# A depthwise convolution and a rotation, each behind a group norm: order of late loads, order of GpSimd's work, place of small matrix products, and a tile without padding

## The chip, the cores and the metric

One core of one Trainium2 chip. The metric is the device time of one execution in microseconds (us), the median of several runs. The kernel is written by hand for five engines: PE (TensorE), DVE (VectorE), ACT (ScalarE), POOL (GpSimd) and SP (SyncE, which here only issues DMAs). They meet in semaphores alone.

## The reference, cut to what matters

```python
x = x + conv5x5_depthwise(group_norm(x), kernel(weight))   # x: (16, 128, 64, 64) f32, pad 2, 32 groups of 4 channels
x = x + einsum('hvc,bchw->bvhw', R, group_norm(x))         # R: (64, 128, 128), one matrix per image row h
```

The group norm takes mean and variance over 4 channels and one whole image, so the second norm of a group can be had only when the first line is done for that group, and the rotation mixes all 128 channels, so it begins when all 32 groups are done.

## The kernel before

**First stage: 32 groups of four channels.** A group holds 4 channels of 16 images. On the 128 partitions lie the 64 rows of images 0 to 7 (low half) and of images 8 to 15 (high half); the free dimension is image, channel, column. The vertical part of the convolution is a banded 64x64 matrix (`taps`), one per channel and per column offset d of 0 to 4; the horizontal part is the shift of the moving operand by d. So `convolve(k, pair, d)` (L560) issues four matrix products of 64x64 by 512 columns for a pair of channels, one in each quadrant of the array, and five offsets add up in PSUM: 2 pairs x 5 offsets x 4 products in a group. The profile shows each f32 product as two records, so 80 records in a group. The moving operand is `padded` (L91), images of 68 columns with two columns of zeros on each side, which four memsets at the start (L308 to L310) write once.

The steps run s = -3 to 34 on all engines, each with its part of several groups:

- SP loads x for group s+5 (`load_half`, L196: 8 DMAs of 128 KB, in pieces of 256 bytes) into a ring of 7 once `x1_ready` frees the slot; after steps 11, 18 and 25 of its loop it stores norms (`store_norms`, L228), and at steps ROT_STEP = 24 to 27 it issues one fourth of the rotation matrices each (L253 to L256, 1 MB each).
- DVE measures group s+3 (`measure`, L484, four `bn_stats` at L489), from step FILL = 4 on ahead of the rest of the step and before that behind it; makes scale and shift of group s+1 (L509, L511); adds the second pair of group s-1 to x (`add`, L473: L478 reads PSUM, L481 reads two SBUF tiles) and measures the sum (L496); makes the variance term of round s+2 (`dev`, `dev2`, `spread`, L522 to L527); adds the first pair of group s.
- PE convolves group s, and between its products puts the small products that average over partitions: `average_spread(s+1)` (L578, the variance) at the first two offsets of the first pair, `average_mean(s+2)` (L584) in the second pair, at the first two offsets, or the last two while 0 <= s < FILL. PE takes instructions in order, so a small product that waits holds all behind it.
- ACT takes the root (L418), normalises five of the eight image pairs (L423), evicts two channels of each group (L407) and stores the sum of a group as two DMAs of 512 KB on its own queue (L207).
- POOL builds the banded matrices of group s+2 (`spread_taps`, L327, four instructions at L339, one per channel) and normalises the other three image pairs (`normalise`, L349, three instructions at L354). From step FILL on it does the four matrices first.

**Between the stages.** Once the sums of groups 0 to 27 are stored (the waits at L265), SP loads the first seven units of the second stage for these 112 channels (`early`, L266 to L269: 7 DMAs of 896 KB). It stores the last group (L272), waits until all sums are stored (L276), and loads the remaining 16 channels of these units (`late`, L282). All of SP's DMAs go through one queue, in order; ACT's stores go through another.

**Second stage.** 32 units of 4 image rows: load (L301), normalise (ACT L448, POOL L383, DVE L539 for the first unit), one 128x128 by 512 product per row (PE L632), add to x (DVE L549), store as 15 DMAs of 2 MB and two of 1 MB (L287). PE's own turning of the rotation matrices (L617) starts when they have landed (L608).

Of the kernel before, what the change touches and what calls it, by code (L numbers as in the profile page):

```python
# [10 lines left out]
B, C, H, W = 16, 128, 64, 64  # L11
GC = 4
# [7 lines left out]
PAD = 2  # L20
WP = W + 2 * PAD
# [39 lines left out]
ROT_STEP = GROUPS - 8  # L61

def conv_rotate_kernel(nc, x, weight, rota, out):
# [5 lines left out]
    with ExitStack() as ctx:  # L70
# [20 lines left out]
        padded = [piece((GC, J, WP)) for _ in range(GRING)]  # L91
# [214 lines left out]
        def _(pool):  # L306
            nc.gpsimd.memset(eps[:], EPS).then_inc(consts_ready, 1)
            for t in padded:  # L308
                nc.gpsimd.memset(t[:, :, :, 0:PAD], 0.0).then_inc(consts_ready, 1)
                nc.gpsimd.memset(t[:, :, :, W + PAD:WP], 0.0).then_inc(consts_ready, 1)  # L310
# [16 lines left out]
            def spread_taps(k):  # L327
# [5 lines left out]
                if k >= TRING:  # L333
                    pool.wait_ge(convolved, 2 * (k - TRING + 1))
                of_rows = mask[:].rearrange("p (b r) -> p b r", r=TAPS)
                for c in range(GC):
                    at = (k * GC + c) * KW
                    of_taps = row_taps[:, :, at:at + KW].rearrange("p r d -> p d r")
                    last = nc.gpsimd.tensor_tensor(  # L339
                        taps[k % TRING][:, c * KW:(c + 1) * KW].rearrange("p d (b r) -> p d b r", r=TAPS),  # L340
                        bass.AP(tensor=of_rows.tensor, offset=of_rows.offset,
                                ap=[of_rows.ap[0], [0, KW], *of_rows.ap[1:]]),
                        bass.AP(tensor=of_taps.tensor, offset=of_taps.offset,
                                ap=[*of_taps.ap[:2], [0, BLOCKS], of_taps.ap[2]]),
                        ALU.mult)
                    if c % 2 == 1:
                        last.then_inc(taps_ready, 1)

            def normalise(k):  # L349
# [3 lines left out]
                for j in range(POOL_J):  # L353
                    last = nc.gpsimd.tensor_scalar(padded[k % GRING][:, :, j, PAD:PAD + W], xin[k % XRING][:, j],  # L354
# [10 lines left out]

            for s in STEPS:
                if group(s + 1) and 0 <= s < FILL:
                    normalise(s + 1)
                if group(s + 2):
                    spread_taps(s + 2)  # L370
                if group(s + 1) and s >= FILL:
                    normalise(s + 1)
                if s - 3 in range(LAST, GROUPS):
                    send_norms(s - 3)
# [14 lines left out]
        def _(act):  # L389
# [21 lines left out]
            for s in STEPS:  # L411
# [7 lines left out]
                if group(s + 1):  # L419
                    k = s + 1  # L420
                    act.wait_ge(affine_ready, k + 1)
                    for j in range(POOL_J if k else 0, J):
                        last = nc.scalar.activation(padded[k % GRING][:, :, j, PAD:PAD + W], xin[k % XRING][:, j],  # L423
# [130 lines left out]
        def _(pe):  # L554
            pe.wait_ge(consts_ready, 1 + 2 * GRING)
# [4 lines left out]
            def convolve(k, pair, d):  # L560
                bank = 2 * ((2 * k + pair) % PAIRS)
                if d == 0:
# [5 lines left out]
                    if 2 * k + pair >= PAIRS:  # L568
                        pe.wait_ge(y_ready, (2 * k + pair - PAIRS + 1) * 2)
                        pe.wait_ge(own_ready, 2 * k + pair - PAIRS + 1)  # L570
                for rows, half, c in ((low, low, 0), (low, high, 1), (high, low, 1), (high, high, 0)):
                    last = nc.tensor.matmul(ps[half, bank + c], taps[k % TRING][rows, (2 * pair + c) * KW + d, 0:H],  # L572
                                            padded[k % GRING][rows, 2 * pair + c, :, d:d + W],
                                            start=(d == 0), stop=(d == KW - 1))
                if d == KW - 1:
# [17 lines left out]

            for s in STEPS:
                first = KW - 2 if 0 <= s < FILL else 0
                for d in range(KW):
                    if group(s):
                        convolve(s, 0, d)
                    if is_round(s + 1) and d < 2:
                        average_spread(s + 1, high if d else low)  # L600
                for d in range(KW):
                    if group(s):
                        convolve(s, 1, d)
                    if is_round(s + 2) and d in (first, first + 1):
                        average_mean(s + 2, low if d == first else high)
# [55 lines left out]
```

## Time and profile before

| | us |
|---|---|
| median of 3 runs | 499.12 (496.28 to 499.28) |
| the profiled execution, its own time | 498.91 |
| its span, first to last instruction | 497.1 |
| PE busy | 425.3 |
| DVE busy | 369.6 |
| ACT, POOL busy | 259.2, 256.6 |

The span is told in microseconds from the first instruction. The mean granted clock of PE is 0.949 of full speed. The page's slices of PE show it at 1.0 in most of the first stage. Busy shares are averages over both stages; what bounds the kernel has to be read stage by stage.

### The profile page before, as it was taken

How to read it: one execution, taken by the hardware profiler on the slowest of the kernel's cores; microseconds unless marked ns; L12 is line 12 of the kernel's file. 1: busy time of each engine (PE TensorE's matmuls, PEld its weight loads, DVE VectorE, ACT ScalarE, POOL GpSimd, SP SyncE). 2: the span in 40 equal slices, each digit the busy share in tenths (PEclk: the TensorE clock that was granted, in tenths of full speed). 3: DMA queues.
4: the chain of work that ended last, by engine and by line, in shares of the span. 5: the costliest groups of instructions: out<-in, count | busy, mean ns of one | idle time of the engine just before them, and what ended most of it. 6: DMA issues, size and time to landing. Idle time of an engine off the chain costs nothing.

```text
span 497.1 us, 8820 instructions
## 1 busy us (share of the span) xinstructions
PE 425.3 (86%) x3168; PEld 229.9 (46%) x3168; DVE 369.6 (74%) x716; ACT 259.2 (52%) x502; POOL 256.6 (52%) x348
## 2 busy tenths in 40 slices
PE   0199979999999999999999959945999979788972
PEld 0145535556655666556665535523444434333430
DVE  3419999999999999999999856663777643355462
ACT  1344536565565655656556535424777746364640
POOL 3484586675766757667576634213344423132320
PEclk9999998999999999999999979975999989798987
DMA  9989999999999999899999998996999999999998
GB/s 135 182 181 229 211 211 233 249 236 245 250 216 250 230 243 258 210 248 220 244 241 275 273 246 223 341 339 97 390 411 419 407 415 417 415 415 414 415 404 282
DMA packets 180443, 140.70 MB, mean 283 GB/s; under 512 B 139760, under 2 KB 141872, under 8 KB 176304
## 3 DMA queue, kind: packets, MB, share of 16 engines
q1 hardware_dynamic: 159264, 106.86, 76.8%
q10 hardware_dynamic: 20656, 33.16, 23.6%
q8 instruction: 25, 0.41, 0.3%
q0 software_dynamic: 480, 0.11, 0.2%
q14 instruction: 18, 0.15, 0.1%
HBM read 72.96 MB, written 67.15 MB: 282 GB/s over the span
## 4 chain that ended last, share of the span: by engine, by line
DVE 44%; PE 23%; DMA 22%; issue 4%; SPq 2%; POOL 1%; ACTq 1%; ACT 0%; POOLq 0%; DVEq 0%
DMA out_dram<-area 18%; PE ps L572 14%; DVE stats L489 12%; DVE stats L496 12%; DVE area L481 9%; PE ps L632 8%; DVE area L478 4%; DVE area L549 2%; SPq L198 2%; DMA tap_rows<-line 2%; DVE dev L525 1%; DMA area<-in_x_dram 1%; DVE affine L511 1%; DVE affine L509 1%; DMA area<-tap_rows 1%
## 5 line engine op out<-in xcount | busy, mean ns | idle before, releaser
L572 PE MATMUL ps<-area 64*64 64x512 f32 x2560 | 292.7, 607 | 3.9 <-POOL area L339 3.9
L572 PEld LDWEIGHTS ps<-area 64*64 64x64 f32 x2560 | 160.5, 134 | 92.8 <-issue 54.9
L339 POOL TENSOR_TENSOR area<-mask,area 128x325 f32<-128x325 f32 x128 | 130.3, 1054 | 76.5 <-PE ps L572 71.4
L632 PE MATMUL ps<-area 128*128 128x512 f32 x256 | 123.6, 635 | 20.4 <-DVE area L549 16.0
L549 DVE TENSOR_TENSOR area<-ps,area 128x512 f32<-128x512 f32 x128 | 82.9, 687 | 61.3 <-DMA out_dram<-area 46.2
L407 ACT ACTIVATE area<-ps 64x512 f32<-64x512 f32 x128 | 75.8, 592 | 72.1 <-PE ps L572 69.8
L448 ACT ACTIVATE area<-area,norm 128x256 f32<-128x256 f32 x157 | 80.5, 588 | 55.8 <-PE ps L632 54.1
L423 ACT ACTIVATE area<-area,affine 128x256 f32<-128x256 f32 x163 | 83.7, 590 | 42.0 <-DVE affine L511 42.0
L383 POOL TENSOR_SCALAR area<-area,norm 128x256 f32<-128x256 f32 x95 | 52.0, 562 | 91.7 <-PE ps L632 88.5
L489 DVE BATCH_NORM_STATS2 stats<-area 128x6 f32<-128x512 f32 x128 | 80.4, 690 | 18.1 <-DMA area<-in_x_dram 18.1
L632 PEld LDWEIGHTS ps<-area 128*128 128x128 f32 x256 | 50.2, 204 | 82.8 <-issue 48.0
L496 DVE BATCH_NORM_STATS2 stats<-area 128x6 f32<-128x512 f32 x128 | 80.7, 693 | 1.1
L354 POOL TENSOR_SCALAR area<-area,affine 128x256 f32<-128x256 f32 x93 | 64.1, 702 | 27.2 <-DVE affine L511 27.2
L481 DVE TENSOR_TENSOR area<-area 128x512 f32<-128x512 f32 x64 | 59.8, 934 | 0.0
L478 DVE TENSOR_TENSOR area<-ps,area 128x512 f32<-128x512 f32 x64 | 43.6, 682 | 0.0
L589 PE MATMUL ps<-stats,half_mean 64*64 64x16 f32 (+1 forms) x144 | 17.2, 200 | 28.6 <-DVE affine L511 16.0
L589 PEld LDWEIGHTS ps<-stats,half_mean 64*64 64x64 f32 x144 | 18.9, 142 | 45.5 <-issue 30.6
L418 ACT ACTIVATE std<-ps,eps 128x16 f32<-128x16 f32 (+1 forms) x36 | 9.8, 273 | 50.7 <-PE ps L581 34.7
L581 PEld LDWEIGHTS ps<-spread,half_mean 64*64 64x64 f32 x144 | 18.2, 140 | 26.6 <-issue 15.0
L581 PE MATMUL ps<-spread,half_mean 64*64 64x16 f32 (+1 forms) x144 | 16.7, 198 | 8.0 <-DVE spread L527 8.0
L509 DVE RECIPROCAL affine<-std 128x16 f32<-128x16 f32 (+1 forms) x36 | 8.2, 227 | 15.1 <-ACT std L418 15.1
L362 POOL DMA_DIRECT2D norm<-affine x8 | 4.1, 521 | 20.1 <-DVE affine L511 19.8
(27 smaller groups left out, 68.7 us busy)
## 6 DMA issues: line engine op xcount, KB each, us to landing
area<-in_x_dram SPq DMA_DIRECT2D x252, 128.0 KB, 4.3
x_scratch<-area ACTq DMA_DIRECT2D x62, 512.0 KB, 6.2
out_dram<-area SPq DMA_DIRECT2D x15, 2048.0 KB, 17.9
area<-x_scratch SPq DMA_DIRECT2D x25, 1024.0 KB, 14.6
area<-x_scratch SPq DMA_DIRECT2D x7, 896.0 KB, 13.8
out_dram<-area SPq DMA_DIRECT2D x2, 1024.0 KB, 9.1
area<-tap_rows SPq DMA_DIRECT2D x8, 142.2 KB
x_scratch<-area SPq DMA_DIRECT2D x2, 512.0 KB, 5.6
```

What stands on the lines that cost most here:

```text
L339: last = nc.gpsimd.tensor_tensor(taps[k % TRING][:, c * KW:(c + 1) * KW].rearrange("p d (b r) -> p d b r", r=TAPS), bass.AP(tensor=of_rows ...
L354: last = nc.gpsimd.tensor_scalar(padded[k % GRING][:, :, j, PAD:PAD + W], xin[k % XRING][:, j], affine[:, k, 0, 0, j:j + 1], affine[:, k, ...
L407: last = nc.scalar.activation(y[k % YRING][rows, 2 * pair + 1], ps[half, bank + 1].rearrange("p (j w) -> p j w", j=J), ACT.Identity)
L423: last = nc.scalar.activation(padded[k % GRING][:, :, j, PAD:PAD + W], xin[k % XRING][:, j], ACT.Identity, scale=affine[:, k, 0, 0, j:j + ...
L448: last = nc.scalar.activation(gn[n % NRING][:, :, j], tin[n % IRING][:, :, j], ACT.Identity, scale=norm2[:, unit_half(n)[1], 0, j:j + 1], ...
L478: nc.vector.tensor_tensor(y[k % YRING][:, c], ps[:, bank].rearrange("p (j w) -> p j w", j=J), xin[k % XRING][:, :, c], ALU.add).then_inc(o ...
L481: nc.vector.tensor_tensor(y[k % YRING][:, c + 1], y[k % YRING][:, c + 1], xin[k % XRING][:, :, c + 1], ALU.add).then_inc(x1_ready, 1)
L489: last = nc.vector.bn_stats(out=stats[:, k % 2, 0, 2 * q:2 * q + 2].rearrange("p j f -> p (j f)"), in_=xin[k % XRING][:, 2 * q:2 * q + 2]. ...
L496: last = nc.vector.bn_stats(out=stats[:, (k + 4) % 2, 1, 2 * q:2 * q + 2].rearrange("p j f -> p (j f)"), in_=y[k % YRING][:, :, 2 * q:2 * ...
L549: nc.vector.tensor_tensor(tout[slot][:, :, rows + h], ps[:, (n * RH + h) % 6, :].rearrange("p (j w) -> p j w", j=J), tin[n % IRING][:, h], ...
L572: last = nc.tensor.matmul(ps[half, bank + c], taps[k % TRING][rows, (2 * pair + c) * KW + d, 0:H], padded[k % GRING][rows, 2 * pair + c, : ...
L632: nc.tensor.matmul(ps[:, m % 6, :], rot_t[u % TURNED][:, h], gn[n % NRING][:, h], start=True, stop=True).then_inc(rotated, 1)
```

## The change

Five edits:

1. ROT_STEP goes from GROUPS - 8 to GROUPS - 5, so the rotation matrices are issued at steps 27 to 30, behind the last load of x (step 26).
2. POOL's four matrix instructions of a step are cut in two calls: channels 0 and 1, then (from step FILL on) the three images, then channels 2 and 3. The waits ahead of them go into a function of their own. In steps 0 to 3 the images stay ahead of all four.
3. PE's `average_spread` goes in steps 1 to 3 from the first two offsets to the last two; both small products stand at positions 2 and 3 in step 4, at 1 and 2 in step 5, and at 0 and 1 from step 6. Low and high half change places in `average_spread`.
4. `padded` becomes `normed` without the zero columns. The middle offset comes first and covers all 512 columns; the outer ones leave out the columns that the zeros fed: 496 columns for d = 0 and 4, 504 for d = 1 and 3.
5. With the padding go its four memsets and PE's wait for them; the work area is laid out 256 elements shorter.

```diff
-WP = W + 2 * PAD
+OFFSETS = (PAD, 0, 1, 3, 4)
-ROT_STEP = GROUPS - 8
+ROT_STEP = GROUPS - 5
-        padded = [piece((GC, J, WP)) for _ in range(GRING)]
+        normed = [piece((GC, J, W)) for _ in range(GRING)]
-            for t in padded:
-                nc.gpsimd.memset(t[:, :, :, 0:PAD], 0.0).then_inc(consts_ready, 1)
-                nc.gpsimd.memset(t[:, :, :, W + PAD:WP], 0.0).then_inc(consts_ready, 1)
...
             for s in STEPS:
                 if group(s + 1) and 0 <= s < FILL:
                     normalise(s + 1)
                 if group(s + 2):
-                    spread_taps(s + 2)
+                    await_taps(s + 2)
+                    spread_taps(s + 2, (0, 1))
                 if group(s + 1) and s >= FILL:
                     normalise(s + 1)
+                if group(s + 2):
+                    spread_taps(s + 2, (2, 3))
...
-                if d == 0:
+                if d == OFFSETS[0]:
...
+                shift = d - PAD
+                outs, ins = slice(max(0, -shift), W - max(0, shift)), slice(max(0, shift), W + min(0, shift))
                 for rows, half, c in ((low, low, 0), (low, high, 1), (high, low, 1), (high, high, 0)):
-                    last = nc.tensor.matmul(ps[half, bank + c], taps[k % TRING][rows, (2 * pair + c) * KW + d, 0:H],
-                                            padded[k % GRING][rows, 2 * pair + c, :, d:d + W],
-                                            start=(d == 0), stop=(d == KW - 1))
+                    last = nc.tensor.matmul(ps[half, bank + c].rearrange("p (j w) -> p j w", j=J)[:, :, outs],
+                                            taps[k % TRING][rows, (2 * pair + c) * KW + d, 0:H],
+                                            normed[k % GRING][rows, 2 * pair + c, :, ins],
+                                            start=(d == OFFSETS[0]), stop=(d == OFFSETS[-1]))
...
+            def place(s):
+                return min(KW - 2, max(0, FILL + KW - 3 - s)) if s >= 0 else 0
+
             for s in STEPS:
-                first = KW - 2 if 0 <= s < FILL else 0
-                for d in range(KW):
+                first, first_spread = place(s), place(s) if s >= 1 else 0
+                for at, d in enumerate(OFFSETS):
                     if group(s):
                         convolve(s, 0, d)
-                    if is_round(s + 1) and d < 2:
-                        average_spread(s + 1, high if d else low)
-                for d in range(KW):
+                    if is_round(s + 1) and at in (first_spread, first_spread + 1):
+                        average_spread(s + 1, low if at == first_spread else high)
+                for at, d in enumerate(OFFSETS):
                     if group(s):
                         convolve(s, 1, d)
-                    if is_round(s + 2) and d in (first, first + 1):
-                        average_mean(s + 2, low if d == first else high)
+                    if is_round(s + 2) and at in (first, first + 1):
+                        average_mean(s + 2, low if at == first else high)
```

## Rows read from the trace of the kernel before

**Rows 1.** The page of before, GB/s by slice (part 2), chain by engine (part 4)
```profile
GB/s 135 182 181 229 211 211 233 249 236 245 250 216 250 230 243 258 210 248 220 244 241 275 273 246 223 341 339 97 390 411 419 407 415 417 415 415 414 415 404 282
...
DVE 44%; PE 23%; DMA 22%; issue 4%; SPq 2%; POOL 1%; ACTq 1%; ACT 0%; POOLq 0%; DVEq 0%
```

**Rows 2.** Timeline of DVE: start, microseconds, instruction, count, idle before
```profile
251.64 1.32 DVE L481 TENSOR_TENSOR area<-area 128x512 f32<-128x512 f32 x1
...
274.29 0.68 DVE L481 TENSOR_TENSOR area<-area 128x512 f32<-128x512 f32 x1
274.88 2.53 DVE L489 BATCH_NORM_STATS2 stats<-area 128x6 f32<-128x512 f32 x4
...
291.24 2.50 DVE L489 BATCH_NORM_STATS2 stats<-area 128x6 f32<-128x512 f32 x4 [7.40 <-DMA area<-in_x_dram]
```

**Rows 3.** Timeline of POOL, one step
```profile
248.35 4.06 POOL L339 TENSOR_TENSOR area<-mask,area 128x325 f32<-128x325 f32 x4 [2.76 <-PE ps L572]
```

**Rows 4.** Timeline of PE, end of the convolutions
```profile
301.17 0.18 PE L581 MATMUL ps<-spread,half_mean 64*64 64x16 f32 x1
...
310.05 0.18 PE L581 MATMUL ps<-spread,half_mean 64*64 64x16 f32 x1
...
325.60 1.58 PE L572 MATMUL ps<-area 64*64 64x512 f32 x12
```

**Rows 5.** Timeline of SyncE's queue, 24 to 345
```profile
142.94 58.56 SPq L198 DMA_DIRECT2D area<-in_x_dram  x56
...
205.16 53.81 SPq L198 DMA_DIRECT2D area<-in_x_dram  x48
...
260.25 10.88 SPq L198 DMA_DIRECT2D area<-in_x_dram  x8
271.17 0.93 SPq L232 DMA_DIRECT2D norm_scratch<-affine  x2
...
273.94 12.80 SPq L198 DMA_DIRECT2D area<-in_x_dram  x8
287.19 3.53 SPq L256 DMA_DIRECT2D rot_all<-_L_conv_rota_matrix_dram  x2
301.87 2.51 SPq L260 DMA_DIRECT2D area<-x_scratch  x5
```

**Rows 6.** Busy time by stretch; DMA share and GB/s stand last
```profile
107.00:258.60 151.60, 151.60 (x1505) 91.30 (x1501) 149.26 (x291) 88.96 (x171) 104.74 (x121) 1.00 1.03 237
289.50:295.50 6.00, 1.25 (x10) 0.82 (x14) 4.19 (x9) 1.36 (x3) 1.29 (x2) 0.75 1.06 290
304.00:310.00 6.00, 6.00 (x62) 3.17 (x55) 5.42 (x10) 3.52 (x7) 2.77 (x4) 1.00 1.02 276
313.00:328.00 15.00, 14.24 (x144) 7.64 (x136) 10.17 (x23) 6.25 (x13) 2.39 (x4) 1.00 1.03 325
328.50:337.10 8.60, 1.77 (x16) 1.46 (x16) 5.64 (x18) 0.75 (x3) 2.00 (x4) 0.59 0.92 330
```

**Rows 7.** Loads of x at L198, 203.5 to 259
```profile
DMA to landing us min/median/max: 3.0/4.6/6.9
```

**Rows 8.** Who waited for whom: microseconds, times, longest
```profile
DVE stats L489 <- DMA area<-in_x_dram: 18.1, 4, 7.4
```

**Rows 9.** DMA issues by kind, 300 to 345: count, KB, median landing
```profile
area<-x_scratch SPq DMA_DIRECT2D x7, 896.0 KB, 13.8
x_scratch<-area ACTq DMA_DIRECT2D x6, 512.0 KB, 15.7
```

**Rows 10.** Timeline of DVE and PE, start of the second stage
```profile
341.64 2.04 DVE L539 TENSOR_SCALAR area<-area,norm 128x256 f32<-128x256 f32 x4 [4.49 <-DMA norm<-affine]
...
343.74 2.07 PE L632 MATMUL ps<-area 128*128 128x512 f32 x2 [4.43 <-DVE area L539]
```

**Rows 11.** Timeline of PE, first steps
```profile
46.77 0.22 PE L581 MATMUL ps<-spread,half_mean 64*64 64x8 f32 x1 [0.96 <-DVE spread L527]
...
73.93 0.20 PE L589 MATMUL ps<-stats,half_mean 64*64 64x16 f32 x1 [2.14 <-DVE affine L511]
```

More of the change, by code:

```diff
@@ L325, in _, with await_taps @@
             pool.wait_ge(mask_ready, 2)
-            def spread_taps(k):
+            def await_taps(k):
                 if k < FIRST:
@@ L334, in spread_taps @@
                     pool.wait_ge(convolved, 2 * (k - TRING + 1))
+            def spread_taps(k, cs):
                 of_rows = mask[:].rearrange("p (b r) -> p b r", r=TAPS)
-                for c in range(GC):
+                for c in cs:
                     at = (k * GC + c) * KW
@@ L353, in normalise @@
                 for j in range(POOL_J):
-                    last = nc.gpsimd.tensor_scalar(padded[k % GRING][:, :, j, PAD:PAD + W], xin[k % XRING][:, j],
+                    last = nc.gpsimd.tensor_scalar(normed[k % GRING][:, :, j], xin[k % XRING][:, j],
                                                    affine[:, k, 0, 0, j:j + 1], affine[:, k, 0, 1, j:j + 1],
@@ L422, in _ @@
                     for j in range(POOL_J if k else 0, J):
-                        last = nc.scalar.activation(padded[k % GRING][:, :, j, PAD:PAD + W], xin[k % XRING][:, j],
+                        last = nc.scalar.activation(normed[k % GRING][:, :, j], xin[k % XRING][:, j],
                                                     ACT.Identity, scale=affine[:, k, 0, 0, j:j + 1],
@@ L554, in _ @@
         def _(pe):
-            pe.wait_ge(consts_ready, 1 + 2 * GRING)
+            pe.wait_ge(consts_ready, 1)
             pe.wait_ge(half_mean_ready, 1)
@@ L570, in convolve @@
                         pe.wait_ge(own_ready, 2 * k + pair - PAIRS + 1)
+                shift = d - PAD
+                outs, ins = slice(max(0, -shift), W - max(0, shift)), slice(max(0, shift), W + min(0, shift))
                 for rows, half, c in ((low, low, 0), (low, high, 1), (high, low, 1), (high, high, 0)):
-                    last = nc.tensor.matmul(ps[half, bank + c], taps[k % TRING][rows, (2 * pair + c) * KW + d, 0:H],
-                                            padded[k % GRING][rows, 2 * pair + c, :, d:d + W],
-                                            start=(d == 0), stop=(d == KW - 1))
-                if d == KW - 1:
+                    last = nc.tensor.matmul(ps[half, bank + c].rearrange("p (j w) -> p j w", j=J)[:, :, outs],
+                                            taps[k % TRING][rows, (2 * pair + c) * KW + d, 0:H],
+                                            normed[k % GRING][rows, 2 * pair + c, :, ins],
+                                            start=(d == OFFSETS[0]), stop=(d == OFFSETS[-1]))
+                if d == OFFSETS[-1]:
                     last.then_inc(convolved, 1)
```

## The prediction, on record before the changed kernel ran

> **What bounds the kernel now.** I read the chain that ended last, then who waited for whom, then the timelines of the engines around what these two name. The chain is shared: DVE 44%, PE 23%, DMA 22% [rows 1]. The reader should distrust the first figure, because DVE in the steady steps is slowed rather than full. Its second sum at L481 takes 1.32 us where the first takes 0.68 [rows 2], and it ends half a microsecond after the four matrix instructions of POOL (248.35 + 4.06 = 252.41) [rows 3]. DVE waits there for POOL, and POOL for PE. PE is busy for all of the 151.6 us from 107 to 258.6 [rows 6], and in the last steps, where DVE has time to spare, its period is the same: 310.05 - 301.17 = 8.88 us [rows 4]. So PE sets the steady step, with DVE about 0.6 us behind it.
>
> Close behind both stands a third: the stream of x. SP issues 104 loads (13 groups) in 58.56 + 53.81 = 112.4 us without a pause, 8.64 us a group [rows 5], at a DMA share of 1.03 [rows 6]; a load lands 4.6 us after its issue [rows 7]. Group 30 is issued until 260.25 + 10.88 = 271.13 and lands when DVE measures it at 274.88; group 31, with the first two parts of the rotation matrices in front of it, is issued until 286.74, and DVE stands 7.40 us for it [rows 2, 5]. That is all that x costs DVE in the steady part; the other three of its four waits for x (18.1 us together [rows 8]) lie ahead of the first product.
>
> Between the stages the DMA decides again. The early units are issued at 301.87 [rows 5]; from there to 337 the engines are full at 276 to 330 GB/s [rows 6], and ACT's stores of 512 KB take 15.7 us in the median to land [rows 9]. The second stage begins at 341.64 with DVE, at 343.74 with PE [rows 10], and is DMA work at about 415 GB/s [rows 1].
>
> **The change part by part.** *Shorter outer offsets.* They leave out 16 + 8 + 8 + 16 = 48 of 2560 columns, 1.9% of the step without its small products (8.88 - 0.35, an estimate: two small products in each half, of two records of 0.18 us [rows 4] that overlap by half): 0.16 us a step, PE's period 8.72. Bounds: +0.3 us a step, if strided columns cost as much as they save twice over, and -0.16. I take -0.16: the rows of 64 were strided already (68 apart). The four memsets write 256 columns together, where one matrix instruction writes 325 in 1.0 us [rows 3]: bounds -1 and 0; I take 0, since the stream of x doesn't begin with them.
>
> *Variance late in steps 1 to 3.* PE waits 0.96 us for the variance term at 46.77, and twice more alike, and 2.14 us at 73.93 for the mean [rows 11]. Moved to the last two offsets, the variance waits no longer. What is late next is DVE: its step in the ramp is nearly full (two sums, two measures, the terms), so a step gives back about 1 us and not more. With the positions 2 and 3 in step 4, half of the 2.14 stays. I take 3.2 us and 1.0 for the columns of six steps: 4.2 by step 6. Bounds 0 and 5.1 (3 x 0.96 + 2.14).
>
> *Images between two pairs of matrices.* No work is added. L481 loses up to 0.64 us of waiting, and DVE's terms behind the measured sum meet the second pair instead. Bounds for DVE: -0.64 and +0.6 us a step. PE is the slower one and hides either, up to a DVE period of 8.9; the matrices, which come some 2 us later, are used a step later.
>
> *Rotation matrices behind x.* This moves four DMAs of 1 MB past two groups of x, one store of norms, and none of POOL's or ACT's queue. Without them: group 29 is issued until 258.97; 8.64 for group 30; 2.3 for the norms (0.93 in the row, 3.66 in the gap between the first two rows); 8.64 for group 31: 278.6, landed 283.2 [rows 5, 7]. Since the ramp puts the sums 4 us earlier, up to half a store more (of 1 MB, 3.6 us at 290 GB/s [rows 6]) is carried before then: 1.1 us. Group 31 lands at 284.3, not 291.24: 6.9 us earlier. The gain of the ramp and of the columns doesn't add to this. DVE alone would be at group 31 at 283.8 (274.88 + 8.88) - 4.2 - 3.4 (21 steps of 0.16) = 276.2, but x isn't there. DVE will therefore wait a little in many steps.
>
> From there PE needs 2.5 us of measuring, 0.4 for scale and shift, and four offsets (3.9): step 29 starts near 291.1, against 300.2 (one offset ahead of 301.17 [rows 4]); of the old delay some 2 us were the granted clock, 0.75 in 289.5 to 295.5 [rows 6], half at 1.2 GHz. Three steps of 8.72 end the products at 317.3, against 325.60 + 1.58 = 327.2 [rows 4]: 9.9 us earlier.
>
> *What takes this back.* From 284.3 the DMA has in front of it the rotation matrices whole, 4 x 3.6 = 14.4 us; before, half of them had gone while x had a lead. With the store of group 27 (2.7, partly beside them) the early units start at 301.4, as they did (301.87). They are 7 x 896 KB = 6.42 MB [rows 9] at 276 GB/s, the rate with nothing beside them [rows 6]: 23.3 us, to 324.7. Beside them the stores get about 55 GB/s (325 against 276, a little more once they are queued): 1.3 MB. Groups 28 to 30 are 3.15 MB, of which 0.3 goes before; with the last group's 1.05 remain 2.6 MB at 330 GB/s [rows 6], 7.9 us: all sums stored at 332.6, against 337.1. The rest of the way is as before: the late parts, the normalised unit, the second stage. So 4.5 us of 9.9 remain. Span 497.1 - 4.5 = 492.6; the execution has 1.8 more (498.91 against 497.1), 494.4 us. The profiled execution is 0.2 below the median of 499.12, which I leave out.
>
> **Rivals.** *A: the end of the products decides (17%).* For it: if the stores share better than 55 GB/s, the early units no longer hold them. From the end of the products to DVE's start lay 341.64 - 327.2 = 14.4 us, with the norms' own DMAs in it; the whole 9.9 us would stay: 489.0 us. Against it: the 15.7 us of the stores [rows 9].
>
> *B: no change (16%).* All DMA work is the same and only its order is new. Full engines from 107 to 337 [rows 6] mean that only idle time between can be won: some 3 us around 300, where nothing but the store of group 27 was on its way. If x lands at 288 and not at 284, that too is used up: 498 to 499. By that alone the time would stay near 499; the shares of 1.0 agree with it, the lower rates between the stages don't.
>
> *C: slower (12%).* The mechanism is the whole 4 MB standing between x and the early units on one queue in order. By the sum above all sums are stored 332.6 - 284.3 = 48.3 us after group 31 has landed, so it breaks even at 337.1 - 48.3 = 288.8. If the earlier stores slow x as much as the matrices did, x lands at 291.2 again and the last sum at 339.5: 2.4 us later, 501.3, and over 504 where the matrices share with two stores. For it: the last x loads took 12.80 us beside one part of the matrices [rows 5], so the stream gives way easily. Against it: x's own rate of 8.64 was taken with a store in each group.
>
> *D: the forecast (55%)*, 491.5 to 497.0. It covers x landing between 281.5 and 286.5.
>
> **How the numbers follow.** A measurement of this kernel tells about 1% (5 us) from no change; 494.1 is that bound. Half of D lies below it (0.26), and nearly all of A: faster 0.43. The other part of D, B and half of C give same 0.50; the rest of C gives slower 0.07. The range runs from 488.8, which takes in most of A, to 500, which leaves out C.
>
> **What would show it.** Right: the four issues of L256 in one run behind the last x near 279; DVE's waits for x spread over steps 10 to 28 in pieces under 2 us, none of 7; PE's wait for the variance gone in steps 2 to 4 and step 6 some 4 us earlier; products ended near 317; the early units issued near 301 although the products are 10 us ahead; DVE's first L539 near 337. Half records of outer offsets shorter by 2 to 3% and a period of 8.72 in steps 29 to 31. Wrong: x waits that sum to nothing (then the stream is faster than I take it), early units issued before 297, or a first L539 at 332 (A) or behind 342 (C).

## The result and the profile after

The changed kernel takes 506.13 us in the median of four executions (504.36 to 507.76), the kernel before 499.2; the ratio is 1.0158 with an interval of 1.0098 to 1.0218. It is slower by 1.6% where I had forecast 1% faster, and outside my range of 488.8 to 500. The profiled execution took 504.36 us, its span is 502.1.

In e2, e4, e5 and e8 below the executions scatter over 8 us or more, and a ratio is formed only from those near the fastest, so the median of all executions stands beside it.

The page of the changed kernel, busy time, share and count by engine, the chain that ended last by engine (answers to [rows 1]), and one of its costliest groups:

```profile
PE 420.0 (84%) x3168; PEld 212.6 (42%) x3168; DVE 384.8 (77%) x716; ACT 259.2 (52%) x502; POOL 254.6 (51%) x344
...
DVE 48%; DMA 23%; PE 17%; issue 8%; POOL 1%; ACTq 1%; ACT 0%; SPq 0%; POOLq 0%; DVEq 0%
...
L530 DVE SCALAR_TENSOR_TENSOR spread<-stats,dev 128x16 f32<-128x16 f32 (+1 forms) x36 | 28.2, 783 | 1.2
```

PE is less busy than before, DVE by 15 us more, and DVE has 48% of the chain instead of 44, PE 17% instead of 23. The 36 variance terms take 783 ns each on average, although the work is 16 numbers a partition or less; before, those of 16 numbers took 231 ns.

One step in the timeline of DVE in the changed kernel (answers to [rows 2]):

```profile
257.50 0.17 DVE L525 TENSOR_TENSOR dev<-stats,ps 128x16 f32<-128x16 f32 x1
257.70 0.33 DVE L528 TENSOR_TENSOR dev<-dev 128x16 f32<-128x16 f32 x1
258.06 0.95 DVE L530 SCALAR_TENSOR_TENSOR spread<-stats,dev 128x16 f32<-128x16 f32 x1
...
259.54 1.00 DVE L484 TENSOR_TENSOR area<-area 128x512 f32<-128x512 f32 x1
260.47 2.49 DVE L492 BATCH_NORM_STATS2 stats<-area 128x6 f32<-128x512 f32 x4
...
269.97 2.50 DVE L492 BATCH_NORM_STATS2 stats<-area 128x6 f32<-128x512 f32 x4
```

And of POOL in the same step (answers to [rows 3]):

```profile
253.93 2.06 POOL L353 TENSOR_SCALAR area<-area,affine 128x256 f32<-128x256 f32 x3 [3.44 <-DVE affine L514]
255.95 4.04 POOL L338 TENSOR_TENSOR area<-mask,area 128x325 f32<-128x325 f32 x4
```

The step is 269.97 - 260.47 = 9.50 us, against 8.88 before. DVE has no idle time in it; its second sum no longer waits (0.68), but `dev2` (L528) takes 0.34, `spread` (L530) 0.96 and the first pair's sum (L484) 1.00 us. All three begin inside 255.95 to 259.99, where POOL now makes four matrices in a row: the second pair of one group and the first pair of the next, behind the images, which wait for DVE. PE is no longer the bound; it stands 0.54 us a step for DVE's variance term:

```profile
259.07 0.23 PE L588 MATMUL ps<-spread,half_mean 64*64 64x16 f32 x1 [0.54 <-DVE spread L530]
```

The wait of 7.40 us for x has gone, as forecast: the three that are left lie ahead of the first product, and group 31, issued until 282.92, is measured at 298.53. The small waits that I had forecast in many steps aren't there either; with steps of 9.50 us DVE asks for x later than it lands. The waits and SyncE's queue of the changed kernel ([rows 5, 8]):

```profile
DVE stats L492 <- DMA area<-in_x_dram: 12.1, 3, 5.0
```

```profile
274.26 8.66 SPq L198 DMA_DIRECT2D area<-in_x_dram  x8
283.39 11.58 SPq L256 DMA_DIRECT2D rot_all<-_L_conv_rota_matrix_dram  x4
309.13 2.67 SPq L260 DMA_DIRECT2D area<-x_scratch  x5
```

So what the loads gave (7.4 us), and the little that the first steps gave, was paid back by some 23 steps of 0.63 us more, 14.5 us: DVE comes to group 31 at 298.53 and not at 291.24, and the early units are issued at 309.13 and not near 301. PE in the second stage (answers to [rows 10]):

```profile
348.40 5.07 PE L642 MATMUL ps<-area 128*128 128x512 f32 x7 [4.36 <-DVE area L542]
```

It begins 4.7 us later than before (343.74), where I had expected it 4.5 us earlier.

### The profile page after: what moved, and what is told of

Read it like the earlier page. It is cut to its first block, busy times and chain, and to the rows that moved or that the text cites. A ratio compares the mean times of both kernels' runs of the same rounds, so it can differ in the third digit from the quotient of the medians.

```text
span 502.1 us, 8816 instructions
## 1 busy us (share of the span) xinstructions
PE 420.0 (84%) x3168; PEld 212.6 (42%) x3168; DVE 384.8 (77%) x716; ACT 259.2 (52%) x502; POOL 254.6 (51%) x344
## 4 chain that ended last, share of the span: by engine, by line
DVE 48%; DMA 23%; PE 17%; issue 8%; POOL 1%; ACTq 1%; ACT 0%; SPq 0%; POOLq 0%; DVEq 0%
DMA out_dram<-area 18%; DVE stats L499 14%; DVE stats L492 14%; DVE area L484 9%; PE ps L642 8%; PE ps L578 8%; DVE area L481 4%; DVE area L552 2%; DVE dev L528 2%; DMA tap_rows<-line 2%; DMA x_scratch<-area 1%; DMA area<-tap_rows 1%; DVE affine L514 1%; DVE affine L512 1%; ACTq L221 1%
## 5 line engine op out<-in xcount | busy, mean ns | idle before, releaser
L578 PE MATMUL ps<-area 64*64 64x496 f32 (+2 forms) x2560 | 288.5, 591 | 5.7 <-POOL area L338 4.3
L578 PEld LDWEIGHTS ps<-area 64*64 64x64 f32 x2560 | 147.9, 134 | 93.7 <-issue 84.5
L642 PE MATMUL ps<-area 128*128 128x512 f32 x256 | 122.0, 627 | 22.0 <-DVE area L552 17.6
L484 DVE TENSOR_TENSOR area<-area 128x512 f32<-128x512 f32 x64 | 52.5, 820 | 0.0
L588 PEld LDWEIGHTS ps<-spread,half_mean 64*64 64x64 f32 x144 | 16.7, 140 | 46.6 <-DVE spread L530 42.3
L596 PEld LDWEIGHTS ps<-stats,half_mean 64*64 64x64 f32 x144 | 16.5, 138 | 46.1 <-DVE stats L492 26.3
L588 PE MATMUL ps<-spread,half_mean 64*64 64x16 f32 (+1 forms) x144 | 17.8, 206 | 19.5 <-DVE spread L530 19.5
L530 DVE SCALAR_TENSOR_TENSOR spread<-stats,dev 128x16 f32<-128x16 f32 (+1 forms) x36 | 28.2, 783 | 1.2
```

Source lines behind the costliest of these rows:

```text
L484: nc.vector.tensor_tensor(y[k % YRING][:, c + 1], y[k % YRING][:, c + 1], xin[k % XRING][:, :, c + 1], ALU.add).then_inc(x1_ready, 1)
L578: last = nc.tensor.matmul(ps[half, bank + c].rearrange("p (j w) -> p j w", j=J)[:, :, outs], taps[k % TRING][rows, (2 * pair + c) * KW + d ...
L642: nc.tensor.matmul(ps[:, m % 6, :], rot_t[u % TURNED][:, h], gn[n % NRING][:, h], start=True, stop=True).then_inc(rotated, 1)
```

## The experiments

Twelve kernels were run. Each was timed beside the kernel before on the same chip, whose median there was 497.7 to 498.8 us.

### One part undone, or one part alone

**e1_order_back**: the changed kernel with all four matrices ahead of the images again.

```diff
-                    spread_taps(s + 2, (0, 1))
+                    spread_taps(s + 2, (0, 1, 2, 3))
                 if group(s + 1) and s >= FILL:
                     normalise(s + 1)
-                if group(s + 2):
-                    spread_taps(s + 2, (2, 3))
```

> The changed kernel with one edit undone: from step 4 on POOL makes all four matrices ahead of the images again. Theory (POOL's order): DVE's terms (dev2, spread) and its first-pair L484-type sum no longer meet POOL's matrices; the terms fall from 0.34 and 0.96 us to 0.18 each, the DVE step from 9.52 us to 8.9 or less (PE at 8.72), and the time to 492 to 497 us, about what was forecast for the whole change. Rival 1 (the late variance put the engines out of phase): the step stays near 9.5 us and the time at 504 to 506. Rival 2 (shorter offsets cost PE more than they save): the step is above 8.88 with DVE idle, time 500 or more.

503.45 us, ratio 1.015 (1.0074 to 1.0226). My theory fell: with POOL's old order the steps are 9.40 us, so the split by itself is not the cause, and the first rival is nearer.

**e2_split_alone**: the kernel before with that split and nothing else.

```diff
-                    spread_taps(s + 2)
+                    await_taps(s + 2)
+                    spread_taps(s + 2, (0, 1))
...
+                if group(s + 2):
+                    spread_taps(s + 2, (2, 3))
```

> The kernel before with the split of POOL's order alone. Theory (POOL's order): steps of about 9.5 us from step 5 on, 21 x 0.64 = 13.4 us more, of which the 7.4 us wait for the last x is taken back since x then arrives in time: 503 to 507 us. Rivals (phase from the ramp, or the offsets): the split hides behind PE as I first took it, step 8.88, 498 to 500 us.

The median is 507.2 us (four executions: 499.69, 507.03, 507.37, 509.4; ratio 1.0144, 1.0007 to 1.0281), but the profiled one took 499.69, and in it the split does just what it was meant to. Timeline of DVE in that execution:

```profile
242.27 0.25 DVE L514 RECIPROCAL affine<-std 128x16 f32<-128x16 f32 x1 [0.35 <-ACT std L423]
...
243.25 0.69 DVE L486 TENSOR_TENSOR area<-area 128x512 f32<-128x512 f32 x1
...
246.62 0.35 DVE L530 TENSOR_TENSOR dev<-dev 128x16 f32<-128x16 f32 x1
247.00 0.17 DVE L532 SCALAR_TENSOR_TENSOR spread<-stats,dev 128x16 f32<-128x16 f32 x1
```

The second pair's sum (L486) takes 0.69 us, `spread` (L532) 0.17, and DVE even idles 0.35 us in a step of 8.88. Near the end of the same execution, behind a wait of 3.26 us for x, POOL makes four matrices in a row (from 283.29) and one `spread` beside them, at 285.40, takes 0.97 us. So what differs is not what is done but when. This run is inconclusive for the theory as I had put it, and its other executions, 7 to 10 us longer, were not profiled.

**e3_rot_alone**: the kernel before with the late rotation loads and nothing else.

```diff
-ROT_STEP = GROUPS - 8
+ROT_STEP = GROUPS - 5
```

> The kernel before with the rotation matrices behind the last x alone. Theory (my sum of the DMA work): no 7.4 us wait for x, products end 8 to 9 us earlier, early units issued near 301, stores drained near 333 to 335; 494 to 497 us. Rival (the 4 MB stand in front of the early units and take it all back or more): 499 to 503 us. Rival (products decide, nothing taken back): 489 to 491 us.

496.32 us, ratio 0.9981 (0.9944 to 1.0017): on the faster side, within what can be told from nothing. SyncE's queue, and PE at the start of the second stage, in this kernel:

```profile
269.18 8.76 SPq L198 DMA_DIRECT2D area<-in_x_dram  x8
278.41 12.71 SPq L256 DMA_DIRECT2D rot_all<-_L_conv_rota_matrix_dram  x4
298.99 4.52 SPq L260 DMA_DIRECT2D area<-x_scratch  x5
...
317.53 0.30 PE L581 MATMUL ps<-spread,half_mean 64*64 64x8 f32 x4
...
340.42 6.58 PE L632 MATMUL ps<-area 128*128 128x512 f32 x8 [10.68 <-DVE area L539]
```

Group 31 is issued until 277.94 (my sum: 278.6), the products end near 317.8, 9.4 us earlier than before, the early units go out at 298.99, and PE begins at 340.42 instead of 343.74: 3.3 of 9.4 us remain. Before that it had stood 10.68 us for DVE, and DVE 10.73 us for the load of its first unit. The sum of the DMA work between the stages was right to about 1 us: DVE begins at 338.32, where I had 337.1.

**e4_offsets_alone**: the kernel before with the tile without padding and the short offsets.

```diff
-WP = W + 2 * PAD
+OFFSETS = (PAD, 0, 1, 3, 4)
...
-        padded = [piece((GC, J, WP)) for _ in range(GRING)]
+        normed = [piece((GC, J, W)) for _ in range(GRING)]
...
-                    last = nc.tensor.matmul(ps[half, bank + c], taps[k % TRING][rows, (2 * pair + c) * KW + d, 0:H],
-                                            padded[k % GRING][rows, 2 * pair + c, :, d:d + W],
+                    last = nc.tensor.matmul(ps[half, bank + c].rearrange("p (j w) -> p j w", j=J)[:, :, outs],
+                                            taps[k % TRING][rows, (2 * pair + c) * KW + d, 0:H],
+                                            normed[k % GRING][rows, 2 * pair + c, :, ins],
```

> The kernel before with the tile without padding and the shorter outer offsets alone (late variance, POOL's order and the rotation loads as before). Theory: PE's period where it sets the step is 8.72 instead of 8.88, but the last x lands as before, so the wait for it grows by what the steps gain: 498 to 499.5 us. Rival (strided short products cost more): period 8.9 or more, 500 to 504 us. Rival (x isn't near its limit): 494 to 496 us.

501.18 us, ratio 1.0095 (1.0043 to 1.0146). The profiled execution took 495.86 us, with steps of 8.66 us and DVE waiting 9.6 us for the last two groups of x; the ten executions reach from there to 503.88. The short products cost PE nothing: 0.22 us a step are saved, more than my 0.16. Yet this edit alone makes the median worse, above what I had expected, and not by the rival's mechanism, whose steps were 8.9 us or more.

**e5_var_back**: the changed kernel with the small products of the first steps where they were.

```diff
-                first, first_spread = place(s), place(s) if s >= 1 else 0
+                first, first_spread = (KW - 2 if 0 <= s < FILL else 0), 0
```

> The changed kernel with the small products of the first steps where they were (variance at the first two offsets). Theory (two phases: with the variance late PE runs ahead of DVE in steps 1 to 4, DVE's terms then fall beside POOL's matrices, cost 0.8 us more, and DVE with 9.4 to 9.5 us a step never catches up; PE's old wait kept DVE in front): dev2 and spread at 0.35 and 0.18 us, steps of 8.66 to 8.8, DVE idle before its reciprocal, and 491 to 496 us. Rival (the split of POOL's order is the cause by itself): steps stay at 9.5, 504 to 507.

499.47 us, ratio 0.9994 (0.9955 to 1.0032). The mechanism is as expected in the profiled execution (497.3 us): 8.66 us a step, `dev2` about 0.35 and `spread` 0.18 us. Timelines of DVE and POOL in it:

```profile
243.01 0.32 DVE L528 TENSOR_TENSOR dev<-dev 128x16 f32<-128x16 f32 x1
243.36 0.18 DVE L530 SCALAR_TENSOR_TENSOR spread<-stats,dev 128x16 f32<-128x16 f32 x1
...
241.26 2.04 POOL L338 TENSOR_TENSOR area<-mask,area 128x325 f32<-128x325 f32 x2
```

The second pair stands alone here, as the prediction took it, and `spread` starts behind it. Steps in which DVE catches up after a wait for x take 8.43 us (`spread` at 174.67 and 183.10): that is DVE's whole need in this order. Between 227 and 276 us four waits for x of 0.63 to 1.01 us use up DVE's lead; from 278.38 on POOL makes four in a row, and two `spread` (280.49 and 290.00) take 0.96 us. So the changed kernel's order of work can run in either way. The time was expected too low; three of ten executions lie at 504.8 to 506.93.

**e6_var_alone**: the kernel before with the late variance and nothing else.

```diff
-                first = KW - 2 if 0 <= s < FILL else 0
+                first = min(KW - 2, max(0, FILL + KW - 3 - s)) if s >= 0 else 0
+                first_spread = first if s >= 1 else 0
...
-                    if is_round(s + 1) and d < 2:
-                        average_spread(s + 1, high if d else low)
+                    if is_round(s + 1) and d in (first_spread, first_spread + 1):
+                        average_spread(s + 1, low if d == first_spread else high)
```

> The kernel before with the late variance alone. Theory (two phases): the ramp gives 0.6 us in each of steps 1 to 3, then steps of 9.4 us with spread at 0.96 to 1.0 us although POOL's order is the old one; the wait for the last x is gone and the time 503 to 507 us. Rival (it needs the split or the shorter offsets too): steps 8.88, 496 to 499 us.

498.8 us, ratio 0.9995 (0.9964 to 1.0026). My expectation was wrong and the rival right: with full offsets the late variance does no harm. Why is in the timelines. DVE and POOL in this kernel, steps 6 and 7 of PE:

```profile
88.24 0.96 DVE L527 SCALAR_TENSOR_TENSOR spread<-stats,dev 128x16 f32<-128x16 f32 x1
...
97.58 0.18 DVE L527 SCALAR_TENSOR_TENSOR spread<-stats,dev 128x16 f32<-128x16 f32 x1
...
97.71 2.51 POOL L339 TENSOR_TENSOR area<-mask,area 128x325 f32<-128x325 f32 x2 [2.03 <-PE ps L572]
```

The same in e1_order_back, which has the short offsets:

```profile
86.69 0.96 DVE L528 SCALAR_TENSOR_TENSOR spread<-stats,dev 128x16 f32<-128x16 f32 x1
...
96.03 1.00 DVE L528 SCALAR_TENSOR_TENSOR spread<-stats,dev 128x16 f32<-128x16 f32 x1
...
95.96 4.51 POOL L338 TENSOR_TENSOR area<-mask,area 128x325 f32<-128x325 f32 x4 [1.83 <-PE ps L576]
```

In both a contended `spread` (0.96 us) ends, at 89.20 and 87.65, and PE, which had waited for it, goes on. DVE comes to its next `spread` 8.38 us later in both. POOL's matrices wait for PE's products; with full offsets they start 8.51 us after, 0.13 us behind `spread`, with short ones 8.31 us after, 0.07 us ahead of it. In the first case `spread` takes 0.18 us, DVE is quick again and its lead grows to 0.41 us within a few steps. In the second it takes 1.00 us, PE waits again, and the next step is the same: 9.40 us to the end of the stage. In the kernel before, `spread` starts 1.4 us ahead of the matrices of 248.35 [rows 3]:

```profile
246.95 0.18 DVE L527 SCALAR_TENSOR_TENSOR spread<-stats,dev 128x16 f32<-128x16 f32 x1
```

### What is slowed, and what cures it

**e7_terms_one_input**: the changed kernel without any two-input term. Left out is the squared deviation of each row's mean from the group's.

```diff
-                    nc.vector.tensor_tensor(dev2[:, k], dev[:, k], dev[:, k], ALU.mult).then_inc(dev2_ready, 1)
+                    nc.vector.tensor_scalar(dev2[:, k], dev[:, k], 1.0, None, ALU.mult).then_inc(dev2_ready, 1)
...
-                    nc.vector.scalar_tensor_tensor(out=spread[:, k], in0=stats[:, r % 2, k, :, 2],
-                                                   scalar=1.0 / (GC * W), in1=dev2[:, k], op0=ALU.mult, op1=ALU.add
-                                                   ).then_inc(spread_ready, 1)
+                    nc.vector.tensor_scalar(spread[:, k], stats[:, r % 2, k, :, 2], 1.0 / (GC * W), None, ALU.mult
+                                            ).then_inc(spread_ready, 1)
```

> The changed kernel in which dev2 copies dev instead of squaring it and spread takes the scaled variance without adding dev2, so that neither reads two tensors in SBUF (left out: the squared deviation of each row's mean). Theory (DVE waits for POOL only where it reads two SBUF tensors): both at 0.2 us or less although POOL's matrices still run beside them, the DVE step shorter by 0.9 to 1.0 us, thus 8.7 at most, and 491 to 497 us. Rival (any DVE instruction beside POOL's two-input ones is slowed, or PE's wait decides): dev2 and spread keep 0.3 and 0.9, or the step stays above 9.2; 502 or more.

505.96 us, ratio 1.0151 (1.0097 to 1.0204). Timeline of DVE in it:

```profile
258.55 0.35 DVE L528 TENSOR_SCALAR dev<-dev 128x16 f32<-128x16 f32 x1
258.94 0.96 DVE L530 TENSOR_SCALAR spread<-stats 128x16 f32<-128x16 f32 x1
```

As slow as with two inputs: my rule was too narrow. The Trainium skill has the wider one (GPSIMD Engine Reference, "Key points"): GpSimd shares its SBUF interfaces with VectorE and contends with instructions that have two SBUF inputs or run in a two-port mode. By the Trainium skill's page VectorE: DVE Perf Modes ("Mode 2×_2P — use both read ports for one tensor"), an f32 `tensor_scalar` in SBUF runs in such a mode; by the Trainium skill's same page ("Why PSUM operands drop a tier"), one with a PSUM operand can't. These rows agree with it, and so does `dev` (L525), which reads PSUM and one SBUF tensor and takes 0.17 us in the midst of POOL's matrices.

**e8_offsets_and_rot**: short offsets and late rotation loads, the rest as before. Against e4_offsets_alone:

```diff
-ROT_STEP = GROUPS - 8
+ROT_STEP = GROUPS - 5
```

> Shorter offsets and late rotation loads together, variance and POOL's order as before. Theory: steps of 8.66, no wait for the last x above 3 us, products end near 316, early units at 299, and the stores drain at 332 to 334; 491 to 495 us in the good phase, 500 to 504 in executions that fall into the other. Rival (nothing to be had beyond the late rotations alone): 496 us, as that run.

The median of ten executions is 502.83 us, one of them took 568.36, which nothing here explains; the two fastest are 492.66 and 497.37 (ratio 0.9925, 0.9852 to 0.9998, from these). The profiled one, 497.37, shows the tipping itself. DVE and POOL in it:

```profile
209.57 0.17 DVE L528 SCALAR_TENSOR_TENSOR spread<-stats,dev 128x16 f32<-128x16 f32 x1
...
218.42 0.18 DVE L528 SCALAR_TENSOR_TENSOR spread<-stats,dev 128x16 f32<-128x16 f32 x1
...
222.67 2.50 DVE L490 BATCH_NORM_STATS2 stats<-area 128x6 f32<-128x512 f32 x4 [2.61 <-DMA area<-in_x_dram]
...
229.60 1.00 DVE L528 SCALAR_TENSOR_TENSOR spread<-stats,dev 128x16 f32<-128x16 f32 x1
...
239.01 1.00 DVE L528 SCALAR_TENSOR_TENSOR spread<-stats,dev 128x16 f32<-128x16 f32 x1
...
209.76 4.52 POOL L338 TENSOR_TENSOR area<-mask,area 128x325 f32<-128x325 f32 x4 [2.09 <-PE ps L576]
...
218.42 4.53 POOL L338 TENSOR_TENSOR area<-mask,area 128x325 f32<-128x325 f32 x4 [1.91 <-PE ps L576]
...
229.54 4.50 POOL L338 TENSOR_TENSOR area<-mask,area 128x325 f32<-128x325 f32 x4 [1.84 <-PE ps L576]
...
238.94 4.51 POOL L338 TENSOR_TENSOR area<-mask,area 128x325 f32<-128x325 f32 x4 [1.83 <-PE ps L576]
```

DVE's lead, the time from the start of `spread` to that of POOL's matrices, had run down before: 1.63 us at 78.26, 0.67 at 157.15, 0.19 at 209.57. With short offsets DVE at first takes 8.72 us a step and PE 8.66, so the lead shrinks by 0.06 us in each even without a wait; then the sum at 157.85 takes 1.56 us, and the lead falls to 0.20 in one step and holds. `spread` of the step at 218.42 takes 0.18 us; POOL starts in the same hundredth. In the next step DVE waits 2.61 us for group 24 of x. From then on POOL starts 0.06 to 0.07 us ahead of `spread`, each `spread` takes 1.00 us, and the steps, 8.65 to 8.73 nearly all until then, stay at 9.40 to the end of the stage: 0.74 us in each step that follows. The wait alone doesn't decide it. In e4_offsets_alone the lead runs down to 0.18 us in the same way and holds there, and its waits of 4.38 and 5.19 us for x leave it at 1.47 and 1.56.

**e9_more_products**: e1_order_back with more work for PE, each small product of the mean issued twice.

```diff
+                nc.tensor.matmul(ps_mean[half, k], half_mean[half], stats[half, r % 2, k, :, 1], start=True, stop=True)
                 nc.tensor.matmul(ps_mean[half, k], half_mean[half], stats[half, r % 2, k, :, 1], start=True, stop=True
                                  ).then_inc(mean_ready, 1)
```

> e1_order_back (short offsets, late variance, late rotations, POOL's old order) with every small product of the mean issued twice, to the same place: two more small products in a step, some 0.17 us more work for PE. Theory (two phases decided by which starts first): in e1 POOL's matrices start 8.31 us after the end of a contended spread and DVE's next spread 8.38 after it, so they collide again and again; with 0.17 us more in PE's step the matrices start at 8.48, behind the spread. Steps then fall from 9.40 to about 8.83 us, spread from 1.00 to 0.18, and the kernel with more work is faster: 494 to 498 us. Rival (DVE is simply full, or the contention doesn't hang on this order): 9.4 us a step or more, 503 to 506 us.

494.97 us, ratio 0.9955 (0.9924 to 0.9986): 8.5 us faster than e1_order_back with 144 more records on PE. Its timelines of DVE and POOL:

```profile
247.68 0.18 DVE L528 SCALAR_TENSOR_TENSOR spread<-stats,dev 128x16 f32<-128x16 f32 x1
...
247.84 4.51 POOL L338 TENSOR_TENSOR area<-mask,area 128x325 f32<-128x325 f32 x4 [2.06 <-PE ps L576]
```

`spread` starts 0.16 us ahead of the matrices and takes 0.18 us. The steps are 8.7 to 8.8 us where there is no wait for x, and none of the ten executions is above 497.5. Two waits for x here, of 3.15 and 0.52 us, leave a lead of 0.16 us and don't tip it. This settles it: what cost the time in e1 was the order of two starts, not the amount of anybody's work.

**e10_terms_in_psum**: the changed kernel, whole, with `dev` and `dev2` in spare columns of PSUM. `dev2` is the deviation times the row's own mean, so that one of its inputs is in SBUF and one in PSUM; averaged over a group this equals the squared deviation, since the deviations sum to zero there.

```diff
-        dev = sb("dev", [P, 2, J])
-        dev2 = sb("dev2", [P, 2, J])
+        dev = ps[:, 6, 4 * J:6 * J].rearrange("p (k j) -> p k j", k=2)
+        dev2 = ps[:, 7, 4 * J:6 * J].rearrange("p (k j) -> p k j", k=2)
...
-                    nc.vector.tensor_tensor(dev2[:, k], dev[:, k], dev[:, k], ALU.mult).then_inc(dev2_ready, 1)
+                    nc.vector.tensor_tensor(dev2[:, k], stats[:, r % 2, k, :, 1], dev[:, k], ALU.mult).then_inc(dev2_ready, 1)
```

> The changed kernel with dev and dev2 in spare columns of PSUM, and dev2 as mean times deviation (its average over the partitions is the same), so that dev2 and spread read one SBUF tensor each through the first port, and none of the two-port forms. Theory (DVE waits for POOL's matrices only where it uses the second SBUF port): dev2 and spread at 0.2 us or less beside POOL's matrices, DVE's step 9.52 - 0.94 = 8.6, so PE or x at 8.66 to 8.8 decides; 491 to 497 us. Rival (any small DVE instruction with its output in SBUF waits for POOL): 0.9 us for spread stays, 9.4 to 9.5 us a step, 503 to 507.

494.67 us in the median of twelve, ratio 0.9944 (0.9913 to 0.9974). DVE and POOL in it:

```profile
244.89 0.18 DVE L528 TENSOR_TENSOR ps<-stats,ps 128x16 f32<-128x16 f32 x1
245.10 0.17 DVE L530 SCALAR_TENSOR_TENSOR spread<-stats,ps 128x16 f32<-128x16 f32 x1
...
245.79 0.95 DVE L484 TENSOR_TENSOR area<-area 128x512 f32<-128x512 f32 x1
...
243.14 4.51 POOL L338 TENSOR_TENSOR area<-mask,area 128x325 f32<-128x325 f32 x4
```

Both terms run at 0.18 and 0.17 us in the midst of POOL's matrices (243.14 to 247.65). Only the sum still waits (0.95), and the steps are 8.5 to 8.7 us. This is the change with its fault mended: 11.5 us under the changed kernel's median, 3.3 us under the kernel before on the same chip. That it meets my forecast of 494.4 us is luck in part: the products end 3.2 us earlier than I had summed (314.1 against 317.3), and DVE's second stage begins only 1.1 us earlier (336.03 against 337.1).

**e11_best_guess**: e8_offsets_and_rot with the terms in PSUM (the diff of e10_terms_in_psum).

> e8_offsets_and_rot with the terms in PSUM as in e10. Theory: the slow phase is gone, so a wait for x doesn't tip the rest of the stage into steps of 9.4 us; all executions at 491 to 497 us, 1% or a little less under the kernel before, since the DMA between the stages takes most of the products' lead back. Rival (the phase has another cause than the terms): medians of 502 as for e8.

494.55 us, ratio 0.9925 (0.989 to 0.996), against 502.83 for e8: none of the executions is above 498.86, the lowest is 490.87; I had expected all at 491 to 497. With the fault mended, POOL's order and the late variance are worth nothing that these runs can tell.

**e12_rot_early**: e10_terms_in_psum with the rotation matrices at steps 24 to 27 again.

```diff
-ROT_STEP = GROUPS - 5
+ROT_STEP = GROUPS - 8
```

> e10_terms_in_psum with the rotation matrices issued where the kernel before has them (steps 24 to 27). Theory (what the late rotations give is DMA order alone): group 31 lands near 289 to 291, DVE waits 9 to 13 us for x in all in steps 24 to 28, the products end 7 to 10 us later than in e10, yet the second stage starts only 2 to 4 us later since half of the matrices is gone by then: 495 to 498 us. Rival (the late rotations give nothing once the steps are short): 494 to 495, as e10. Rival (they give all that the products gain): 501 to 504.

497.79 us, ratio 0.9988 (0.9958 to 1.0017): the late rotations are worth 3.1 us beside e10's 494.67, as expected, or 2.2 us by the two ratios, since the chips differ; the two intervals still overlap. The profiled execution took 501.51 us, the longest of the twelve. It has DVE waiting 13.1 us for groups 24, 30 and 31 of x, its products end 14.4 us behind those of e10 (328.5 against 314.1), and PE's second stage begins 7.5 us later (345.42 against 337.88), both more than I had expected.

## Why the prediction was wrong

**The step that failed** is "Images between two pairs of matrices". I wrote "Bounds for DVE: -0.64 and +0.6 us a step. PE is the slower one and hides either, up to a DVE period of 8.9". The term was mis-sized, and so PE didn't hide it. By this change's rows DVE needs 8.88 - 0.64 = 8.24 us with no contention, and then 0.17 (`dev2`) + 0.78 (`spread`) + 0.32 (the first sum) = 9.51, which is the step measured. +1.27 and not +0.6, because I took POOL's second pair to be out of the way after two instructions; behind images that wait for DVE, the next group's first pair follows at once, four in a row. Where the second pair does stand alone (e5), the term is small and hidden, as I wrote: DVE needs 8.43 us. And with the old order (e1) the same miss is there: 0.82 (`spread`) and 0.32 (the sum) on 8.24 give 9.38 us, measured 9.40, and for this meeting the prediction had no term at all.

**And the reasoning behind it.** I treated a step as a sum in which the longest engine hides the others. Here the sum itself depends on the order of two starts. If `spread` comes first, DVE needs about what PE needs (8.72 us against 8.66 at first in e4 and e8, 8.66 later) and keeps its lead or loses it slowly; if POOL comes first, DVE needs more than PE, PE waits for DVE, and POOL, which waits for PE, comes first again. In the kernel before, the lead was 1.4 us. Its DVE had no idle time in a step either: 8.24 us of need and 0.64 of waiting for POOL made the same 8.88 as PE's. I named the 0.6 us by which DVE stands behind PE, but not how far any of the kernel's instructions stands from a collision.

**"Variance late in steps 1 to 3"**: the saving was sought in the right place and taken too large. PE's waits of 0.95 to 1.02 us for the variance went, and the steps there fell from 10.13 and 10.20 us to 9.46 and 9.52 (by the starts of `spread`), 0.67 each where I had about 1. But PE's wait for the mean stayed nearly whole, 2.12 us at 73.19, where I had kept half of 2.14, and the first `spread` of the ramp came 1.1 us later. So the `spread` that step 6 uses starts at 86.82 instead of 87.05: 0.23 us earlier and not 4.2. (The bound of 5.1 us, too, is 5.0 by the terms beside it.) Above all, PE's wait had kept it behind DVE. Without it POOL's matrices, which PE releases, start 1.10 us ahead of `spread` in e1 (76.03 against 77.13), where in the kernel before they start 1.71 us behind it (79.57 against 77.86). Alone this does no harm (e6), with the short offsets it does (e1).

**"Shorter outer offsets"**: 0.22 us a step, not 0.16. Even if the small products cost PE nothing, 1.9% of 8.88 us would be 0.17; where the rest comes from stays open. That gain is what carries POOL's start from 0.13 us behind `spread` to 0.07 us ahead of it.

**"Rotation matrices behind x" and "What takes this back"**: right in the main, as e3 shows: issue until 277.94 against 278.6, products at 317.8, early units at 298.99 against 301.4, and a third of the lead left. e10 shows it again in the quick phase: products end 13 us before those of the kernel before, PE's second stage begins at 337.9, 5.9 us before. In the changed kernel itself none of it could be seen, since DVE measured group 31 at 298.53, long after it had landed. One reading of mine was loose: that group 30 "lands when DVE measures it at 274.88" isn't in the row, which has no wait; it had landed by then.

**The rivals**: C, my slower case, had the wrong mechanism; in e3 the matrices ahead of the early units broke even at worst (interval to 1.0017). B carried a rule on several issuing engines over to the order within one queue, of which the rule doesn't speak; e3's time doesn't exclude it, and e10 beside e12 speaks against it by 2 to 3 us, near the noise. None of the four had DVE and POOL in it, though the row with 1.32 us stood first in my reading. What would have shown me wrong was listed too narrowly for the same reason.

**Still open**: what made e2, e4, e5 and e8 take over 503 us in executions that were not profiled. In the profiled one of e8 the lead had run down and a wait for x came on top; in those of e2 and e5 waits for x tip the last steps. That the longer executions tip in the same way, only earlier, was not shown.

## What to carry to other kernels

Before an edit moves work between engines, look in the trace for instructions that are longer than their shortest copy, and write down the distance of each from the start of what lengthens it, over all steps, since it can shrink from one to the next. Where a slowed engine makes the slowing engine start earlier in relation to it, the loop has two stable phases, and saving 0.2 us on a third engine can cost 0.7 us a step. The mend is to take the instruction out of the contention (here by an operand in PSUM) rather than to tune the distance.

## What the runs showed of the hardware

- A DVE instruction of 16 numbers a partition that reads one or two f32 tensors in SBUF and writes SBUF waits for the POOL instruction under way: 0.95 to 1.07 us instead of 0.18 beside two-input instructions of 1.05 us (after, e1, e6, e7). In the step shown of the changed kernel POOL's four end near 256.96, 257.97, 258.98 and 259.99 (an estimate: quarters of 4.04 us), `dev2` at 258.03 and `spread` at 259.01. With its operands partly in PSUM it takes 0.17 to 0.18 us in the same place (`dev` in after, both terms in e10). `bn_stats` of 512 columns was not slowed: four took 2.49 to 2.54 us with and without POOL's matrices beside them.
- POOL is held up too. Its four matrices take 4.04 us where the sum of 512 columns starts beside the last of them (after), and 4.50 where it falls among them (e1, the sum at 257.29).
- A kernel whose engines meet in semaphores alone can have two speeds, 8.66 and 9.40 us a step with the same instructions. In e8 it switched at a wait of 2.61 us, after the lead had run down from 1.63 to 0.19 us, and stayed so for the rest of the stage; waits of 4.38 and 5.19 us in e4 didn't switch it.
- Leaving columns out of f32 products (496 and 504 of 512) saved at least their share of time (2.5% of a step for 1.9% of the columns), and nothing was lost to the strided output: 8.88 to 8.66 us a step (e4).
